# A graph network's sort pass: the work of three blocks woven turn by turn

## The chip, the cores and the metric

The kernel runs on one core of one Trainium2 chip. The metric is the time of one execution on the device in microseconds (us), the median of several runs. The program uses the five engines of the core: TensorE (PE in the profile, PEld for its weight loads), VectorE (DVE), ScalarE (ACT), GpSimd (POOL) and SyncE (SP), which issues most transfers.

## The reference, cut to what matters

Four graph layers run one after the other on 12,500 nodes and 412,500 edges, sorted by their target `dst`. The change concerns the first message layer alone:

```
def _L0_gnn_ref(node_features, edge_attr_e3nn, ..., edge_index):
    row, col = edge_index[0], edge_index[1]        # src, dst
    x_j = node_features[col]
    m = jnp.einsum('ei,ej,ijh->eh', x_j, edge_attr_e3nn, W_msg_tp) * norm_msg_tp
    m = jax.nn.silu(m)
    m = m @ W_msg_lin * norm_lin
    agg = jax.ops.segment_sum(m, row, num_segments=n_nodes)
    ...
```

Each edge takes its target's features, multiplies them with its eight attributes and the weights, passes through silu, and is added to its source. The later layers read the same edges again.

## The kernel before, in words

`sorted_message` is the sort pass. It computes the messages of this layer, and it also sorts the edges by source and writes the sorted lists that all later edge passes load. The edges come in 104 blocks (`BLOCKS`) of 128 lanes by 31 columns. A node pass ahead of it has multiplied the weights into a table of 128 values per node, so that a message is a gathered row of the table, times the eight attributes, summed over them.

A block goes through these steps, and each engine has its own function for a step, called `place`, `message` and `sum_`:

- `place` (VectorE L838 to L925). From `src` and `dst` each edge gets a cell, one of 34, by its source (L846 to L866). `hot_c` is the one-hot of the cells. `hot_d` (L875) is the one-hot of the target inside a window of 128 nodes, made in eight turns of four columns (`TURNS`). TensorE counts the cells (L1102) and transposes each turn of `hot_d` (L1111) into one bank, `ps_turn`; ScalarE copies it out (L1032). L877 to L901 find the rank of an edge within its cell, with products of 31 by 31; edges past 128 in a cell spill, TensorE counts these (L1114), and L904 to L925 turn rank and cell into a place.
- `message`. TensorE gathers each turn with a matmul of the transposed one-hot and the window (L1125), into two banks in turn. VectorE multiplies with the attributes (L937, one per turn) and sums over them (L943). ScalarE applies silu (L1045) into the record. GpSimd then scatters the records, 31 indirect transfers (L809), one column each, to the sorted places in HBM, and one more for the spills of an earlier block (L823).
- `sum_`. SP loads the sorted slots back (L762) once the scatter has landed, and then, for a later block, the edges' ends (L733 to L735). VectorE splits the messages by three chunks (`thirds`, L951 to L966), makes four groups of one-hots (`HOTS`, L973), and finds repeated spill rows (L977 to L989). TensorE turns two columns of the slots into rows (L1141, L1142), and adds the messages to their sources with 33 products (L1146, each two matmuls), and three more small ones (L1152 to L1156). ScalarE makes a second set of one-hots for the later passes, four groups of Square and Relu (L1063, L1067), and copies the sums out (L1073).

`in_pairs` unrolls the first six blocks and then loops over pairs. In turn k each of these three engines does `place(k)`, then `message(k - 1)`, then `sum_(k - 3)`. The order inside an engine is written out by hand; engines wait for one another by semaphore counts (`Chain` gives each step of each block its number), and a wait holds all that stands behind it on its engine. GpSimd's turn b waits for the index and for the silu of block b. SP's turn k loads the ends of block k, the attributes and the window, clears the records, stores what block k - 4 has ready, and waits for the scatter of block k - 2 to land before it loads its slots.

A copy of the numbers 0 to 127, `ps_iota`, stands in a PSUM bank that also holds accumulators of the first three sum cells; `iota128` is the same in SBUF. The one-hots compare with one of the two.

Of the kernel before, what the change touches and what calls it, by code (L numbers as in the profile page):

```python
# [26 lines left out]
LANES = 128  # L27
# [14 lines left out]
F = 16  # L42
# [68 lines left out]
def _gnn(nc, ctx, ins, out):  # L111
# [491 lines left out]
    def sorted_message(name, table, agg_src, agg_dst, agg_spill):  # L603
# [4 lines left out]
        with ExitStack() as st:  # L608
# [228 lines left out]
            def _(dve):  # L837
                def place(k, x, before):  # L838
# [33 lines left out]
                    if before:  # L872
                        dve.wait_ge(at_.sem, at_.end(k - 1))
                    for t, e in TURNS:
                        dve.tensor_tensor(hot_d[:, t:e, :], bc3(dlo[x][:, t:e], [LANES, e - t, LANES]),  # L875
                                          ps_iota[0:LANES, :].unsqueeze(1).broadcast_to([LANES, e - t, LANES]), ALU.is_equal).then_inc(av.sem, 1)
# [24 lines left out]
                    dve.tensor_reduce(within[:, :], pair[:, :, :], axis=AX.X, op=ALU.add).then_inc(av.sem, 1)  # L901
                    dve.wait_ge(av.sem, av.at("sooner_sum", k))
# [24 lines left out]
                def message(k, x, before):  # L927
# [4 lines left out]
                    dve.wait_ge(attrs_in[x], attrs_of(k, x))  # L932
                    for j, (t, e) in enumerate(TURNS):
                        dve.wait_ge(ct.sem, ct.at(f"gathered{j}", k))
                        if before and j == 0:
                            dve.wait_ge(cv.sem, cv.end(k - 1))
                        dve.tensor_tensor(prod[:, t:e], ps_y[j % 2][0:LANES, 0:(e - t) * AF].rearrange("p (t f a) -> p t f a", f=F, a=A),  # L937
                                          attrE[x][:, t * A:e * A].rearrange("p (t a) -> p t a", a=A).unsqueeze(2)
                                          .broadcast_to([LANES, e - t, F, A]), ALU.mult).then_inc(cv.sem, 1)
# [5 lines left out]
                def sum_(k, x, before):  # L945
# [14 lines left out]
                    message_ = s[:, :, 11:11 + F]  # L960
                    dve.tensor_tensor(thirds[:, :, 2, :], message_, bc3(top[:, :], [LANES, CELLS, F]), ALU.mult).then_inc(bv.sem, 1)
                    dve.tensor_tensor(thirds[:, :, 1, :], message_, bc3(upper[:, :], [LANES, CELLS, F]), ALU.mult).then_inc(bv.sem, 1)
                    dve.wait_ge(bv.sem, bv.at("high", k))
                    dve.tensor_tensor(thirds[:, :, 0, :], message_, thirds[:, :, 1, :], ALU.subtract).then_inc(bv.sem, 1)
                    dve.wait_ge(bv.sem, bv.at("middle", k))
                    dve.tensor_tensor(thirds[:, :, 1, :], thirds[:, :, 1, :], thirds[:, :, 2, :], ALU.subtract).then_inc(bv.sem, 1)  # L966
                    if before >= 2:
                        dve.wait_ge(lists_out[x], per_parity(k, x, 48, -48))
                    for g, (c, e) in enumerate(HOTS):
# [3 lines left out]
                        dve.tensor_tensor(hot[:, c:e, :], bc3(lower[:, c:e], [LANES, e - c, LANES]),  # L973
                                          numbers.unsqueeze(1).broadcast_to([LANES, e - c, LANES]), ALU.is_equal).then_inc(bv.sem, 1)
# [51 lines left out]
            def _(act):  # L1026
# [7 lines left out]
                def message(k, x, before):  # L1034
# [8 lines left out]
                    act.activation(rec[x][:, :, 3:3 + A], attrE[x][:, :].rearrange("p (t a) -> p t a", a=A), ACT.Copy).then_inc(cs.sem, 1)  # L1043
                    act.wait_ge(cv.sem, cv.at("summed", k))
# [3 lines left out]
                def sum_(k, x, before):  # L1048
# [8 lines left out]
                    for g, (c, e) in enumerate(HOTS):  # L1057
                        if g:
                            act.wait_ge(bs.sem, bs.at(f"target{g - 1}", k))
                        elif before:  # L1060
                            act.wait_ge(bs.sem, bs.end(k - 1))
                        for n in range(c, e):
                            last = act.activation(away[:, n - c, :], iota128[:, :], ACT.Square, scale=-1.0, bias=slots[x][:, n, 1:2])  # L1063
                        last.then_inc(bs.sem, 1)
                        act.wait_ge(bs.sem, bs.at(f"away{g}", k))
                        act.activation(ready_[:, :], lane[:, 0:1], ACT.Copy).then_inc(bs.sem, 1)
                        act.activation(targets_[x][:, c * LANES // 2:e * LANES // 2].bitcast(FP8), away[:, 0:e - c, :].rearrange("p c l -> p (c l)"), ACT.Relu,  # L1067
                                       scale=-1.0, bias=1.0, saturate=False).then_inc(bs.sem, 1)
# [27 lines left out]
            def _(pe):  # L1096
                def place(k, x, before):
# [6 lines left out]
                    for j, (t, e) in enumerate(TURNS):  # L1104
                        pe.wait_ge(av.sem, av.at(f"hot_d{j}", k))
                        if j:
                            pe.wait_ge(as_.sem, as_.at(f"turned_out{j - 1}", k))
                        elif before:
                            pe.wait_ge(as_.sem, as_.at(f"turned_out{len(TURNS) - 1}", k - 1))
                        for n in range(t, e):  # L1110
                            mm = pe.matmul(ps_turn[:, (n - t) * LANES:(n - t + 1) * LANES], hot_d[:, n, :], ident16[:, :], start=True, stop=True)  # L1111
                        mm.then_inc(at_.sem, 1)
# [3 lines left out]
                def message(k, x, before):  # L1116
                    pe.wait_ge(attrs_in[x], attrs_of(k, x))
                    pe.wait_ge(as_.sem, as_.end(k))
                    for j, (t, e) in enumerate(TURNS):
                        if j >= 2:  # L1120
                            pe.wait_ge(cv.sem, cv.at(f"prod{j - 2}", k))
                        elif before:
                            pe.wait_ge(cv.sem, cv.at(f"prod{len(TURNS) - 2 + j}", k - 1))
                        for n in range(t, e):
# [2457 lines left out]
```

## Time and profile before

| What | Value |
|---|---|
| Median of 3 runs | 18172.39 us (18166.81 to 18178.23) |
| The profiled execution | 18176.88 us, span 18175.2 us |
| Busy over the span | PE 14091.7, DVE 13399.8, ACT 7133.0, POOL 4607.0 us |
| Mean granted clock of TensorE | 0.814 |
| Sort pass, 1000 to 2000 us of the span | PE 700, DVE 836, ACT 492, POOL 722 us of 1000, clock 0.61 |

The sort pass fills about the stretch from 430 to 5280 us; the first product sum is at 477.0 and the last at 5200.9. Behind it come the node passes and the other edge passes. "Busy" doesn't count waits, semaphore instructions and issue. A granted clock of 1.00 is TensorE's 2.4 GHz level, 0.50 its 1.2 GHz level. A wait is put down to the engine and line whose event came last.

### The profile page before, as it was taken

The page shows a single profiled execution, that of the slowest core. Times are in us where ns is not written, and L with a number is a line of the kernel's source. Part 1 is how long each engine was busy: PE and PEld are TensorE (multiplying, and loading weights), DVE is VectorE, ACT ScalarE, POOL GpSimd, SP SyncE. Part 2 cuts the span into 40 slices and gives each one's busy share as a digit, 9 for nine tenths or more (in the row PEclk, how much of TensorE's full clock was granted, in tenths as well). Part 3 has the DMA queues.
Part 4 walks back from the last instruction along what each step waited for, and adds up shares of the span by engine and source line. Part 5 has one row for each costly group of instructions (what it writes and reads, how often), then busy time and mean ns, then how long its engine had stood idle before and what let it go on. Part 6 is the DMA issues. An engine that isn't in the chain of part 4 may idle for free. (4 is left out here: it accounts for less than half of the span.)

```text
span 18175.2 us, 508933 instructions
## 1 busy us (share of the span) xinstructions
PE 14091.7 (78%) x180600; PEld 12229.2 (67%) x180600; DVE 13399.8 (74%) x32882; ACT 7133.0 (39%) x15316; POOL 4607.0 (25%) x4403
## 2 busy tenths in 40 slices
PE   1676677677667995899999999997699999946565
PEld 0566666666656994777777777776577777736565
DVE  2888888888857995656666666665677777769899
ACT  0444445444432332344444444443344444411111
POOL 0677777777741110011111111110000000001111
PEclk9666666666657996999999999998899999967676
DMA  1122222222213551444444444443344444427566
GB/s 58 53 59 59 58 57 59 59 59 58 59 48 112 156 157 56 107 110 110 110 110 110 110 110 111 110 110 83 108 151 151 151 152 152 144 70 210 169 210 178
DMA packets 1347425, 1956.50 MB, mean 108 GB/s; under 512 B 705453, under 2 KB 923252, under 8 KB 1306316
## 3 DMA queue, kind: packets, MB, share of 16 engines
q1 hardware_dynamic: 1046674, 1621.50, 28.8%
q0 software_dynamic: 209664, 186.01, 7.2%
q10 hardware_dynamic: 90300, 137.10, 2.0%
q8 instruction: 666, 10.91, 0.2%
q14 instruction: 121, 0.99, 0.0%
HBM read 1443.57 MB, written 501.97 MB: 107 GB/s over the span
## 5 line engine op out<-in xcount | busy, mean ns | idle before, releaser
L809 POOL DMA_INDIRECT records<-e_sort_rec,e_sort_index x3224 | 3293.2, 1021 | 1351.1 <-issue 921.2
L2393 PEld LDWEIGHTS e_s_ps_h<-e_s_pick,e_s_parts 128*64 128x64 bf16 x61776 | 2044.1, 116 | 215.7 <-issue 67.6
L2393 PE MATMUL e_s_ps_h<-e_s_pick,e_s_parts 128*64 128x128 bf16 x61776 | 2095.7, 227 | 13.7 <-issue 13.6
L1146 PE MATMUL e_sort_acc<-e_sort_thirds,e_sort_hot 128*128 128x48 f32 x6864 | 1488.7, 414 | 301.0 <-DVE e_sort_hot L973 301.0
L1146 PEld LDWEIGHTS e_sort_acc<-e_sort_thirds,e_sort_hot 128*128 128x128 f32 x6864 | 1472.0, 332 | 331.6 <-DVE e_sort_hot L973 331.6
L2512 POOL DMA_DIRECT2D states<-e_s_second_t x520 | 457.8, 880 | 4603.1 <-ACT e_s_second_t L2241 4531.4
L2029 DVE TENSOR_TENSOR e_s_unit<-e_s_ps_o,lane_out 128x512 f32<-128x512 f32 (+1 forms) x520 | 324.0, 623 | 1720.8 <-PE e_s_ps_o L2351 1720.8
L1989 DVE TENSOR_SCALAR e_s_pick<-e_s_rows,lane_below 128x1024 bf16<-128x1024 bf16 (+1 forms) x3120 | 1178.9, 434 | 232.3 <-PE e_s_ps_h L2393 208.3
L2426 PE MATMUL e_s_ps_o<-w_eblk,e_s_act 128*128 128x128 f32 x7488 | 1018.8, 277 | 210.6 <-DVE e_s_unit L2038 210.6
L2503 POOL DMA_INDIRECT e_s_spill<-send,e_s_lists x208 | 218.5, 1050 | 3677.0 <-PE e_s_ps_h L2415 2757.2
L2426 PEld LDWEIGHTS e_s_ps_o<-w_eblk,e_s_act 128*128 128x128 f32 x7488 | 952.3, 192 | 276.9 <-DVE e_s_unit L2038 230.4
L1063 ACT ACTIVATE e_sort_away<-iota,e_sort_slots 128x128 f32<-128x128 f32 x3640 | 1107.5, 388 | 10.1
L1125 PE MATMUL e_sort_y<-e_sort_window,e_sort_turned 128*128 128x128 f32 x6448 | 997.9, 325 | 11.6 <-DVE e_sort_prod L937 7.5
L1125 PEld LDWEIGHTS e_sort_y<-e_sort_window,e_sort_turned 128*128 128x128 f32 x6448 | 952.3, 234 | 44.6 <-DVE e_sort_prod L937 21.6
L2386 PE MATMUL e_s_ps_h<-e_s_to_hot,e_s_window 128*64 128x512 bf16 (+2 forms) x6240 | 866.9, 383 | 110.0 <-DVE e_s_to_hot L1990 96.1
L2214 ACT ACTIVATE e_s_act<-e_s_ps_h,col_eenc 128x512 f32<-128x512 f32 (+1 forms) x520 | 335.3, 645 | 1533.6 <-PE e_s_ps_h L2342 1533.6
L2453 PE MATMUL e_s_ps_sum<-e_s_unit,e_s_wide 128*128 128x128 f32 x7280 | 899.3, 275 | 0.1
L1111 PE MATMUL e_sort_turn<-ident,e_sort_hot_d 128*128 128x128 bf16 x3224 | 491.6, 306 | 506.0 <-ACT e_sort_turned L1032 498.8
L1400 PE MATMUL e_s_g<-e_s_parts,e_s_pick 128*128 128x48 bf16 x20592 | 768.3, 205 | 120.9 <-DVE e_s_pick_own L1296 64.7
L2453 PEld LDWEIGHTS e_s_ps_sum<-e_s_unit,e_s_wide 128*128 128x128 f32 x7280 | 855.1, 192 | 0.7 <-issue 0.7
L2248 ACT ACTIVATE e_s_act<-e_s_ps_h,col_state 128x512 f32<-128x512 f32 (+1 forms) x1040 | 663.4, 638 | 462.3 <-PE e_s_ps_h L2412 257.5
L1691 PE MATMUL e_s_psp<-e_s_wide,e_s_product 128*128 128x128 f32 x7280 | 839.3, 276 | 3.6 <-DVE e_s_product L1591 3.1
(546 smaller groups left out, 31707.8 us busy)
## 6 DMA issues: line engine op xcount, KB each, us to landing
e_s_rows<-rows_d SPq DMA_DIRECT2D x312, 1088.0 KB, 5.3
e_s_hot<-hots_d SPq DMA_DIRECT2D x520, 560.0 KB, 3.7
e_s_to_rows<-rows_d SPq DMA_DIRECT2D x208, 608.0 KB, 5.7
e_s_rows<-rows_d SPq DMA_DIRECT2D x208, 544.0 KB, 4.3
e_s_rows<-rows_d SPq DMA_DIRECT2D x208, 512.0 KB, 5.2
e_s_to_rows<-rows_d SPq DMA_DIRECT2D x208, 512.0 KB, 6.0
states<-e_s_first_t ACTq DMA_DIRECT2D x416, 256.0 KB, 2.1
states<-e_s_second_t POOLq DMA_DIRECT2D x416, 256.0 KB, 4.0
```

The source lines that it names most:

```text
L809: pool.indirect_dma_start(records, bass.IndirectOffsetOnAxis(ap=index[x][:, t:t + 1], axis=0), rec[x][:, t, :], None,).then_inc(written[x] ...
L1063: last = act.activation(away[:, n - c, :], iota128[:, :], ACT.Square, scale=-1.0, bias=slots[x][:, n, 1:2])
L1125: mm = pe.matmul(ps_y[j % 2][0:LANES, (n - t) * AF:(n - t + 1) * AF], turned[x][:, n, :], window[x][:, :], start=True, stop=True)
L1146: mm = pe.matmul(acc[sum_bank(c)][:, sum_at(c)], hot[:, c, :], thirds[:, c, :, :].rearrange("p h f -> p (h f)"), start=False, stop=last an ...
L1400: mm = pe.matmul(ps_g[g][:, at:at + 3 * F], pick[x][:, h, c * LANES:(c + 1) * LANES], parts[:, SPAN * c + h, :, :].rearrange("p r f -> p ( ...
L1691: mm = pe.matmul(ps_spread[:, 0:LANES], product[x][:, c].rearrange("p a f -> p (a f)"), wide[:, c * LANES:(c + 1) * LANES], start=c == 0, ...
L1989: dve.tensor_scalar(pick[p][:, h, 0:(f - c) * LANES], rows_[:, c * LANES:f * LANES], lane_below[:, h:h + 1], None, ALU.is_equal).then_inc( ...
L2248: act.activation(act1[p][:, 0:turned(s)], hidden_bank(x, s)[:, 0:turned(s)], ACT.Silu, bias=(col_state if enc else col_state1)[:, :]).then ...
L2386: pe.matmul(halves[half][:, 0:n_ * LANES], window[:, r, 1, :], to_pairs[:, half, 0:n_, :], start=r == 0, stop=False, skip_group_check=True)
L2393: mm = pe.matmul(halves[half][:, j * LANES:(j + 1) * LANES], parts[:, SPAN * c + h, r, :], pick[p][:, h, (c - c0) * LANES:(c - c0 + 1) * L ...
L2426: mm = pe.matmul(ps_o1[p % NB][:, j * LANES:(j + 1) * LANES], act1[p][:, j * LANES:(j + 1) * LANES], W[f"eblk1{rnd}"][:, :], start=enc, st ...
L2453: mm = pe.matmul(ps_sum[:, 0:2 * D if enc else D], wide[s][:, (c - c0) * LANES:(c - c0 + 1) * LANES], units_of(x, c), start=c == 0, stop=F ...
```

## The change

The three step functions of VectorE, ScalarE and TensorE are cut into pieces, and the loop bodies call the pieces in a new order. On TensorE each turn gathers block k - 1 and then transposes block k. On VectorE each turn makes a target one-hot of block k and a product of block k - 1, and six of the eight turns also take a piece of the sums of block k - 3. The ranks and places of block k stand at the end. On ScalarE the copies into the record come first, and the silu stands between the second and the third group of target one-hots. One-hot group 2 of the sums reads `iota128` in place of `ps_iota`, and the wait for the first accumulations moves from group 2 to group 3. TensorE's wait for the spill rank moves behind the sums. The same instructions run as before, and the programs of SP and GpSimd are not touched.

```
VectorE:
+                def sum_hot(k, x, g, before):
+                    c, e = HOTS[g]
+                    numbers = iota128[:, :] if g in (1, 2) else ps_iota
+                    if g == 3:
+                        dve.wait_ge(bt.sem, bt.at("early", k))
+                    dve.tensor_tensor(hot[:, c:e, :], bc3(lower[:, c:e], [LANES, e - c, LANES]),
+                                      numbers.unsqueeze(1).broadcast_to([LANES, e - c, LANES]), ALU.is_equal).then_inc(bv.sem, 1)
...
-                        numbers = iota128[:, :] if g == 1 else ps_iota
-                        if g == 2:
-                            dve.wait_ge(bt.sem, bt.at("early", k))
...
                 def body(k, x, before):
                     y = 1 - x
-                    if inside(k):
-                        place(k, x, before)
-                    if before >= 1 and (not isinstance(k, int) or k - 1 < BLOCKS):
+                    new, sent, summed_ = inside(k), before >= 1 and (not isinstance(k, int) or k - 1 < BLOCKS), before >= 3
+                    if new:
+                        cells_(k, x, before)
+                    if sent:
+                        indices(k - 1, y, before - 1)
+                    for j in range(len(TURNS)):
+                        if new:
+                            target_hot(k, x, j, before)
+                        if sent:
+                            products(k - 1, y, j, before - 1)
+                        if summed_ and j == 1:
+                            thirds_low(k - 3, y, before - 3)
+                        if summed_ and j == 2:
+                            thirds_top(k - 3, y, before - 3)
+                        if summed_ and j == 3:
+                            thirds_rest(k - 3, y, before - 3)
+                        if summed_ and j in (4, 5, 6):
+                            sum_hot(k - 3, y, j - 4, before - 3)
+                    if sent:
                         message(k - 1, y, before - 1)
-                    if before >= 3:
-                        sum_(k - 3, y, before - 3)
+                    if summed_:
+                        sum_hot(k - 3, y, 3, before - 3)
+                        spill_rows(k - 3, y, before - 3)
+                    if new:
+                        ranks(k, x, before)
+                        places(k, x, before)
ScalarE:
-                    if inside(k):
+                    if sent:
+                        message(k - 1, y, before - 1)
+                    if new:
                         place(k, x, before)
-                    if before >= 1 and (not isinstance(k, int) or k - 1 < BLOCKS):
-                        message(k - 1, y, before - 1)
-                    if before >= 3:
+                    if summed_:
                         sum_(k - 3, y, before - 3)
+                        targets(k - 3, y, 0, before - 3)
+                        targets(k - 3, y, 1, before - 3)
+                    if sent:
+                        silu_(k - 1, y, before - 1)
+                    if summed_:
+                        targets(k - 3, y, 2, before - 3)
+                        targets(k - 3, y, 3, before - 3)
+                        sums(k - 3, y, before - 3)
TensorE:
-                        pe.wait_ge(av.sem, av.at("spill_rank", k + 3))
...
+                def sum_spills(k, x, before):
+                    if not last_of_places(k):
+                        pe.wait_ge(av.sem, av.at("spill_rank", k + 3))
...
-                    if inside(k):
-                        place(k, x, before)
-                    if before >= 1 and (not isinstance(k, int) or k - 1 < BLOCKS):
-                        message(k - 1, y, before - 1)
-                    if before >= 3:
+                    for j in range(len(TURNS)):
+                        if sent:
+                            message(k - 1, y, j, before - 1)
+                        if new and j == 0:
+                            count(k, x, before)
+                        if new:
+                            turn(k, x, j, before)
+                    if summed_:
                         sum_(k - 3, y, before - 3, isinstance(k, int) and k == BLOCKS + 2)
+                    if new:
+                        spills(k, x, before)
+                    if summed_:
+                        sum_spills(k - 3, y, before - 3)
```

The new functions hold the lines of the old ones unchanged but for what is shown here: on VectorE `cells_`, `target_hot`, `ranks` and `places` are the parts of `place`; `indices`, `products` and `message` those of `message`; `thirds_low`, `thirds_top`, `thirds_rest`, `sum_hot` and `spill_rows` those of `sum_`.

## Rows read from the trace of the kernel before

**Rows 1.** product sum L943 over the stage: count, duration ns, first and last start
```profile
L943 DVE TENSOR_REDUCE e_sort_summed<-e_sort_prod x104: 4285/4286/4287, 477.0 to 5200.9; 128x496 f32<-128x3968 f32 x104
```

**Rows 2.** waits, 500 to 5200: us in total, times, longest
```profile
DVE e_sort_spill_rank L904 <- PE e_sort_misc L1114: 348.7, 100, 4.3
POOL records L809 <- ACT e_sort_rec L1045: 334.1, 102, 5.0
...
DVE e_sort_prod L937 <- PE e_sort_y L1125: 227.1, 569, 11.7
...
DVE e_sort_dlo L846 <- issue: 34.8, 49, 1.4
```

**Rows 3.** groups of GpSimd, 1000 to 5000: busy us, mean ns, idle before
```profile
L809 POOL DMA_INDIRECT records<-e_sort_rec,e_sort_index x2691 | 2750.6, 1022 | 1083.9 <-issue 767.6 <-ACT e_sort_rec L1045 290.4 <-DVE e_sort_index L931 25.9
L823 POOL DMA_INDIRECT agg<-e_sort_merged,e_sort_spill_at x87 | 140.0, 1610 | 26.5 <-issue 26.5
```

**Rows 4.** timeline of VectorE, one block: start us, us
```profile
3004.28 0.18 DVE L951 TENSOR_SCALAR e_sort_upper<-e_sort_slots 128x35 f32<-128x35 f32 x1
...
3009.36 1.35 DVE L973 TENSOR_TENSOR e_sort_hot<-e_sort_lower,iota 128x1152 f32<-128x1152 f32 x1
...
3015.24 0.19 DVE L846 TENSOR_TENSOR e_sort_dlo<-e_sort_dst,e_sort_first 128x31 f32<-128x31 int32 x1
...
3018.29 4.73 DVE L875 TENSOR_TENSOR e_sort_hot_d<-e_sort_dlo,e_sort_acc 128x512 bf16<-128x512 f32 x8
3022.94 1.15 DVE L877 TENSOR_TENSOR e_sort_pair<-e_sort_cell 128x961 f32<-128x961 f32 x1
...
3036.00 0.19 DVE L904 TENSOR_TENSOR e_sort_spill_rank<-e_sort_within,e_sort_misc 128x31 f32<-128x31 f32 x1 [3.70 <-PE e_sort_misc L1114]
...
3038.54 0.69 DVE L937 TENSOR_TENSOR e_sort_prod<-e_sort_y,e_sort_attr 128x512 f32<-128x512 f32 x1
```

**Rows 5.** timeline of TensorE, the same blocks
```profile
3004.81 1.07 PE L1141 MATMUL e_sort_turn<-ident,e_sort_slots 128*35 128x128 f32 x4 [5.45 <-DVE e_sort_diagonal L953]
3005.80 0.80 PE L1142 MATMUL e_sort_turn<-e_sort_diagonal,ones 128*128 128x128 f32 x2
3009.50 14.31 PE L1146 MATMUL e_sort_acc<-e_sort_thirds,e_sort_hot 128*128 128x48 f32 x66 [2.90 <-DVE e_sort_hot L973]
...
3025.47 1.06 PE L1102 MATMUL e_sort_misc<-e_sort_hot_c,earlier 128*128 128x34 bf16 x31 [0.43 <-ACT e_sort_merged L1073]
...
3027.64 0.61 PE L1111 MATMUL e_sort_turn<-ident,e_sort_hot_d 128*128 128x128 bf16 x4 [0.69 <-ACT e_sort_turned L1032]
...
3082.20 3.45 PE L1125 MATMUL e_sort_y<-e_sort_window,e_sort_turned 128*128 128x128 f32 x16
```

**Rows 6.** windows: stretch; PE, PEld, DVE, ACT, POOL busy; clock; DMA share; GB/s
```profile
3085.80:3091.60 5.80, 5.71 (x46) 5.36 (x46) 4.06 (x7) 0.00 (x0) 4.34 (x5) 1.00 0.05 11
```

**Rows 7.** timeline of ScalarE: silu and two target groups
```profile
3004.40 0.65 ACT L1045 ACTIVATE e_sort_rec<-e_sort_summed 128x496 f32<-128x496 f32 x1 [12.94 <-DVE e_sort_summed L943]
...
3006.92 2.72 ACT L1063 ACTIVATE e_sort_away<-iota,e_sort_slots 128x128 f32<-128x128 f32 x9
...
3010.96 2.74 ACT L1063 ACTIVATE e_sort_away<-iota,e_sort_slots 128x128 f32<-128x128 f32 x9
```

**Rows 8.** timelines of GpSimd, SP, VectorE, second round; GpSimd at block of group 4
```profile
521.88 0.95 POOL L809 DMA_INDIRECT records<-e_sort_rec,e_sort_index  x1 [0.31 <-issue]
...
526.56 0.43 SPq L735 DMA_DIRECT2D e_sort_first<-firsts_d  x1
...
529.19 0.19 DVE L846 TENSOR_TENSOR e_sort_dlo<-e_sort_dst,e_sort_first 128x31 f32<-128x31 int32 x1 [15.76 <-DMA e_sort_first<-firsts_d]
...
557.07 4.29 DVE L943 TENSOR_REDUCE e_sort_summed<-e_sort_prod 128x496 f32<-128x3968 f32 x1
...
558.55 0.96 POOL L809 DMA_INDIRECT records<-e_sort_rec,e_sort_index  x1 [0.30 <-issue]
...
3009.81 1.74 POOL L809 DMA_INDIRECT records<-e_sort_rec,e_sort_index  x1 [0.30 <-issue]
```

More of the change, by code:

```diff
@@ L837, in _, with cells_ @@
             def _(dve):
-                def place(k, x, before):
+                def cells_(k, x, before):
                     src_, dst_ = srcE[x][:, :], dstE[x][:, :]
@@ L901, in place, with places @@
                     dve.tensor_reduce(within[:, :], pair[:, :, :], axis=AX.X, op=ALU.add).then_inc(av.sem, 1)
+                def places(k, x, before):
                     dve.wait_ge(av.sem, av.at("sooner_sum", k))
@@ L931, in message, with products @@
                     dve.tensor_copy(index[x][:, :], place_[x][:, :]).then_inc(cv.sem, 1)
[L932 to L939, printed above, removed]
+                def products(k, x, j, before):
+                    t, e = TURNS[j]
+                    if j == 0:
+                        dve.wait_ge(attrs_in[x], attrs_of(k, x))
+                    dve.wait_ge(ct.sem, ct.at(f"gathered{j}", k))
+                    if before and j == 0:
+                        dve.wait_ge(cv.sem, cv.end(k - 1))
+                    dve.tensor_tensor(prod[:, t:e], ps_y[j % 2][0:LANES, 0:(e - t) * AF].rearrange("p (t f a) -> p t f a", f=F, a=A),
+                                      attrE[x][:, t * A:e * A].rearrange("p (t a) -> p t a", a=A).unsqueeze(2)
+                                      .broadcast_to([LANES, e - t, F, A]), ALU.mult).then_inc(cv.sem, 1)
+                def message(k, x, before):
                     dve.wait_ge(cv.sem, cv.at(LAST, k))
@@ L1056, in sum_, with targets, sums @@
                     act.activation(rows_t[x][:, :], ps_rows, ACT.Copy).then_inc(bs.sem, 1)
[L1057 to L1068, printed above, removed]
+                def targets(k, x, g, before):
+                    c, e = HOTS[g]
+                    if g:
+                        act.wait_ge(bs.sem, bs.at(f"target{g - 1}", k))
+                    elif before:
+                        act.wait_ge(bs.sem, bs.end(k - 1))
+                    for n in range(c, e):
+                        last = act.activation(away[:, n - c, :], iota128[:, :], ACT.Square, scale=-1.0, bias=slots[x][:, n, 1:2])
+                    last.then_inc(bs.sem, 1)
+                    act.wait_ge(bs.sem, bs.at(f"away{g}", k))
+                    act.activation(ready_[:, :], lane[:, 0:1], ACT.Copy).then_inc(bs.sem, 1)
+                    act.activation(targets_[x][:, c * LANES // 2:e * LANES // 2].bitcast(FP8), away[:, 0:e - c, :].rearrange("p c l -> p (c l)"), ACT.Relu,
+                                   scale=-1.0, bias=1.0, saturate=False).then_inc(bs.sem, 1)
+                def sums(k, x, before):
                     act.wait_ge(bt.sem, bt.at("merged", k))
@@ L1096, in _, with count @@
             def _(pe):
-                def place(k, x, before):
+                def count(k, x, before):
                     pe.wait_ge(av.sem, av.at("hot_c", k))
@@ L1103, in place, with turn @@
                     mm.then_inc(at_.sem, 1)
[L1104 to L1112, printed above, removed]
+                def turn(k, x, j, before):
+                    t, e = TURNS[j]
+                    pe.wait_ge(av.sem, av.at(f"hot_d{j}", k))
+                    if j:
+                        pe.wait_ge(as_.sem, as_.at(f"turned_out{j - 1}", k))
+                    elif before:
+                        pe.wait_ge(as_.sem, as_.at(f"turned_out{len(TURNS) - 1}", k - 1))
+                    for n in range(t, e):
+                        mm = pe.matmul(ps_turn[:, (n - t) * LANES:(n - t + 1) * LANES], hot_d[:, n, :], ident16[:, :], start=True, stop=True)
+                    mm.then_inc(at_.sem, 1)
@@ L1113, in place, with spills, message @@
+                def spills(k, x, before):
                     pe.wait_ge(av.sem, av.at("lates16", k))
                     pe.matmul(ps_lates, earlier16[:, :], lates16[:, :], start=True, stop=True).then_inc(at_.sem, 1)
[L1116 to L1124, printed above, removed]
[L1125 to L1127 removed]
+                def message(k, x, j, before):
+                    t, e = TURNS[j]
+                    if j == 0:
+                        pe.wait_ge(attrs_in[x], attrs_of(k, x))
+                        pe.wait_ge(as_.sem, as_.end(k))
+                    if j >= 2:
+                        pe.wait_ge(cv.sem, cv.at(f"prod{j - 2}", k))
+                    elif before:
+                        pe.wait_ge(cv.sem, cv.at(f"prod{len(TURNS) - 2 + j}", k - 1))
+                    for n in range(t, e):
+                        mm = pe.matmul(ps_y[j % 2][0:LANES, (n - t) * AF:(n - t + 1) * AF], turned[x][:, n, :], window[x][:, :],
+                                       start=True, stop=True)
+                    mm.then_inc(ct.sem, 1)
```

30 lines of the change are left out of this document (17 added, 13 removed).

## The prediction, made before the run

> **What bounds the kernel now.** The change touches one stage only, the sort pass, so I read that stage and left the chain that ended last aside: it lies wholly in the last node pass. First the spacing of one instruction that runs once for each of the 104 blocks, the product sum at L943 [rows 1]: 103 steps from 477.0 to 5200.9, 45.86 us each. The stage is 4724 us of 18175, so one microsecond off a block is worth 103 us, 0.57% of the kernel.
>
> Then the waits [rows 2], to see which engine is ever full. VectorE waits 3.45 us a block (348.7 over 101 blocks) at L904 for TensorE and 2.25 (227.1) at its products; GpSimd waits 3.3 for ScalarE's silu. Nobody is full: the three take turns in one ring. L846 to L875 makes one-hots, TensorE transposes only when the previous block's sums are through, the gathers come after that, and VectorE's sums after the gathers.
>
> Last, how near each engine is to its own limit. GpSimd [rows 3]: 87 rounds in the stretch, 31 scatters of 1.022 us, one spill of 1.61, and 9.43 us of idle time that is only issue (767.6 + 25.9 + 26.5 over 87). That is 42.72, and the wait for silu, 290.4/87 = 3.34, fills it to 46.06. So GpSimd leaves at most 3.0 us a block to be gained, because a round that waits for nothing still pays one issue step of 0.30. VectorE: 46.06 less its two waits is 40.4.
>
> **What the change does, part by part.** No instruction is added or removed; the order on VectorE, ScalarE and TensorE changes, and one of four sum one-hots (group 2) compares with iota128 in SBUF, where it read the copy in PSUM. SP's and GpSimd's programs stay.
>
> *VectorE with TensorE.* I lay one turn of the new loop along durations of before, from L846 at 0. Cells and the chunk one-hot end at 3.05 (3015.24 to 3018.29) [rows 4], the index cast at 3.25 (L904 to the first product, 2.54, holds the places and this cast; I give the cast 0.2), the first target one-hot (0.58: 4.65 for eight, L875 to L877) at 3.85. TensorE starts its count at 3.1, ends it at 4.2 (1.06), transposes four columns (0.61) until 4.8, and only then, because its queue is in order, gathers group 1. A group of gathers costs 3.45/2 = 1.73 [rows 5], so product 1 can start at 6.5. VectorE is there at 5.1 (two one-hots, one product of 0.69): a stall of 1.4. From turn 1 on each turn also holds a piece of the sums: a third of L951 to L973 (5.08 less one one-hot of 1.35 is 3.7, so 1.25 each) or a sum one-hot. VectorE's turn is then 0.58 + 0.69 + 1.25 = 2.5 and TensorE's 1.73 + 0.61 = 2.34, so VectorE hardly waits; I take 0.2 in all. The product sum (4.29 [rows 1]) ends near 26.5, the fourth one-hot and the spill rows near 29.4, the ranks (L877 to L904, 13.06 less the 3.70 of waiting) near 38.8. TensorE meanwhile: last transpose 22.3, ScalarE's copy 0.7 (the wait ahead of L1111), rows 1.07 + 0.80, sums 14.31, so the spill count comes at 39.2: a stall of 0.4 where 3.45 stood. The places add 2.3 and the loop's jump 0.35 (34.8 of idle time at L846 over 101 blocks [rows 2]): 41.9. By parts it is 40.4 + 1.4 + 0.2 + 0.4 = 42.4. I take 42.0. Bounds of this unknown: 40.4 with no stall, and 1.4 in each of eight turns, 40.4 + 11.2 + 0.4 = 52.0. I stand near the low end, because only turn 0 has no filler between its two products.
>
> I took the slow gather. In a long run of gathers the granted clock stood at 1.00, the 2.4 GHz level, and 46 of them took 5.71 us, 0.124 each [rows 6]; the 16 ahead of them took 3.45, 0.216 each [rows 5]. Woven between transposes and waits the long run is gone. The Trainium skill, "TensorE: Matmul & The Clock Gate", Part 1, says the same as a rule: the throttled clock is the default and sustained activity releases it. By the fast rate TensorE's turn would be 1.0 + 0.6 and the first stall 0.7; VectorE's round would be 41.2 where I have 42.0. Neither sets the end of the sum, as GpSimd will show below.
>
> *ScalarE.* The silu moves behind two groups of target one-hots, 4.04 each (L1063 to the next L1063) [rows 7]. TensorE's rows are there at 24.9 (22.3 + 0.7 + 1.9), so silu (0.65) ends near 24.9 + 8.1 + 0.7 = 33.7, 7 us after its input is there. I give GpSimd 0.7 more to start: 34.4 after L846. Does that hold GpSimd up? When round b ends, SP loads slots and then the next ends, and VectorE may start block b+3. The second round at the start of the stage shows this path: last scatter at 521.88, L735 issued at 526.56, VectorE released at 529.19 [rows 8], 6.4 us after the scatter ended (521.88 + 0.96). The silu follows 34.4 later, 40.8 after the scatter's end, less the spill of 1.9 that ends the round, while GpSimd is busy for 43 with the other block. So it is 2 to 4 us early, and GpSimd goes from round to round. VectorE's spare time will then stand at L846.
>
> *GpSimd is what is late next.* Its round without the silu wait is 42.72 + 0.30 = 43.02. But part of 1.022 is collision. A scatter alone takes 0.96 (558.55); the one at 3009.81 took 1.74 and ended 0.84 after the one-hot with iota128 in SBUF (3009.36 + 1.35 = 3010.71) [rows 4, 8]. The 4.29 us product sum delays nothing: the scatter at 558.55 lies inside the one at 557.07. So operations with two SBUF inputs hold GpSimd, and reductions don't; 31 x (1.022 - 0.96) = 1.9 us a block goes there now. The change adds to this. Group 2 becomes a second 1.35 us blocker, longer than a scatter's step of 1.26, so it always catches one: between 0.09 and 1.35, middle 0.72. And the first pair of thirds, which ran while GpSimd sat waiting for silu, now meets a busy GpSimd: between nothing and 0.74, I take 0.3. GpSimd's own loop jump, hidden so far under the silu wait, is between nothing and VectorE's 0.35; I take 0.15. Round after: 43.02 + 0.72 + 0.30 + 0.15 = 44.2.
>
> The Trainium skill, "SBUF — State Buffer", "Who interferes with whom", states this as a rule that speaks against the change: a VectorE instruction with two SBUF inputs takes the port that GpSimd reads through, for its whole length, and a reduction never does. The trace agrees in both halves, by the 1.74 and the 0.96 above. By the rule alone, each of the blockers could cost its full length.
>
> **Sum.** 103 x 44.2 = 4553 against 4724: 171 us less. Fill and drain keep their work, and the stages behind are untouched. The profiled execution took 18176.9 (span 18175.2), 4.5 above the median of 18172.4, so 18172.4 - 171 = 18001; I say 18,000.
>
> **Rivals.**
> - *GpSimd binds as computed*, with 43.0 to 45.4 a block: 17,878 to 18,125. Chance 0.68.
> - *Few collisions.* If the blockers fall between GpSimd's reads (those measured now are 1.9 of some 6 possible), the VectorE and TensorE ring binds, down to 42.0: 103 x 3.86 = 398 less, 17,775. Against it: the 1.35 us blockers are longer than one step. Chance 0.12.
> - *The weave itself stalls.* Where VectorE and TensorE wait for each other in all eight turns, x more in each, a block takes 42.0 + 8x. It shows from x = 0.28 and ends slower than before from x = 0.53; at the bound of 52.0 a block it is 103 x 6.1 = 630 us more, 18,800. Against it: every turn but the first has a filler longer than the transposes. Chance 0.08.
> - *Slower by the port.* Every blocker caught at its start: two one-hots (2.7), two of the three 1.15 us pair operations (2.3), one of each pair of thirds (1.5), 6.5 a block in place of 1.9: 43.02 + 4.6 + 0.15 = 47.8, 103 x 1.9 = 196 more, 18,370. It decides from 5.1 of collisions. For it: the order repeats each block, so a bad phase repeats too. Against: the same blockers now cost 1.9. Chance 0.07.
> - *The silu stays the wait.* If ScalarE reaches it 4 us later than laid out (rows held up by TensorE), GpSimd waits as now and a block stays at 45.5 to 46.2, the time within 0.2%: 18,172. Chance 0.05.
>
> **Numbers.** A difference of 0.2%, 36 us or 0.35 us a block, is about what a measurement can tell. Faster: 0.68 + 0.12 + 0.03 + 0.01 + 0.01 of the five cases, 0.85; within it: 0.02 + 0.02 + 0.03, 0.07; slower: 0.03 + 0.04 + 0.01, 0.08. The range 17,850 to 18,125 holds the first case and the upper part of the second; below it lies 0.08, above it some 0.12.
>
> **What would show it.** Right: L943 every 44.2 us; GpSimd's wait for ScalarE near nothing and its scatters at a mean of 1.05 to 1.06; VectorE's idle time moved from L904 to L846, behind the load of the ends, some 2 us; the gathers at the slow rate throughout. Wrong: waits at every product (the weave), scatters above 1.12 (the port), or GpSimd still waiting 3 us for silu.

## The result, and the profile after

The changed kernel took 17,838.94 us (17,832.56 to 17,847.32, four runs) against 18,171.61 before (18,166.81 to 18,178.23): a ratio of 0.9816, 95% interval 0.9801 to 0.983. It is faster, by nearly twice the 171 us of the prediction, and lies 11 us below the low end of its range. The profiled span is 17,833.8 us. The same kernel run again in a later comparison gave 17,825.87 (17,797.54 to 17,833.18), 0.9799 [0.9783, 0.9816].

The product sum, now at L954, answers to [rows 1]: one line of its own view, with count, durations in ns, first and last start.

```profile
L954 DVE TENSOR_REDUCE e_sort_summed<-e_sort_prod x104: 4285/4286/4287, 463.6 to 4844.8; 128x496 f32<-128x3968 f32 x104
```

A block takes (4844.8 - 463.6)/103 = 42.54 us, where it took 45.86 and 44.2 was forecast. That is 342 us over 103 blocks, as much as the two profiled spans differ (18175.2 and 17833.8): the stage gave all of it.

The waits from 500 to 4900 us (total, times, longest) and the groups of GpSimd from 1000 to 4500 answer to [rows 2] and [rows 3]:

```profile
DVE e_sort_dlo L846 <- DMA e_sort_first<-firsts_d: 182.6, 89, 6.1
DVE e_sort_prod L946 <- PE e_sort_y L1186: 160.8, 103, 1.6
...
DVE e_sort_spill_rank L910 <- PE e_sort_misc L1174: 20.6, 47, 0.8
POOL records L809 <- ACT e_sort_rec L1088: 11.9, 39, 0.3
```

```profile
L809 POOL DMA_INDIRECT records<-e_sort_rec,e_sort_index x2538 | 2557.1, 1008 | 773.2 <-issue 754.6 <-ACT e_sort_rec L1088 9.4 <-DVE e_sort_prod L946 9.1
L823 POOL DMA_INDIRECT agg<-e_sort_merged,e_sort_spill_at x82 | 146.8, 1790 | 25.0 <-issue 25.0
```

GpSimd no longer waits: its longest "wait" for silu, 0.3, is the issue step that stands ahead of every scatter. Its round is 31 x 1.008 + 1.79 + (773.2 + 25.0)/82 = 31.2 + 1.8 + 9.7 = 42.8, the whole block (42.76 in this stretch; the first blocks of the stage are shorter). VectorE's 3.45 for the spill count has shrunk to 0.2, its waits for gathers from 2.25 to 1.6, and it now idles 1.8 us a block at L846, behind the load of the ends. What differs most from the forecast is the scatters: a mean of 1.008 us, lower than before's 1.022, not 1.05 to 1.06.

The timelines of GpSimd and VectorE in one block show why (start, duration; [rows 4, 8] before):

```profile
3011.67 1.57 POOL L809 DMA_INDIRECT records<-e_sort_rec,e_sort_index  x1 [0.30 <-issue]
3013.55 0.96 POOL L809 DMA_INDIRECT records<-e_sort_rec,e_sort_index  x1 [0.31 <-issue]
...
3027.68 0.96 POOL L809 DMA_INDIRECT records<-e_sort_rec,e_sort_index  x1 [0.30 <-ACT e_sort_rec L1088]
3028.94 1.61 POOL L823 DMA_INDIRECT agg<-e_sort_merged,e_sort_spill_at  x1 [0.30 <-issue]
3030.86 0.97 POOL L809 DMA_INDIRECT records<-e_sort_rec,e_sort_index  x1 [0.30 <-issue]
...
3011.07 1.35 DVE L989 TENSOR_TENSOR e_sort_hot<-e_sort_lower,iota 128x1152 f32<-128x1152 f32 x1
...
3013.53 1.41 DVE L989 TENSOR_TENSOR e_sort_hot<-e_sort_lower,iota 128x1152 f32<-128x1152 f32 x1
...
3026.77 0.63 ACT L1088 ACTIVATE e_sort_rec<-e_sort_summed 128x496 f32<-128x496 f32 x1
```

The first one-hot with `iota128` catches the scatter that starts inside it: it ends at 3013.24, 0.82 after the one-hot's end (3011.07 + 1.35 = 3012.42). The next scatter starts 0.30 later, at 3013.55, and so 0.02 after the second such one-hot. This one it passes: it takes its 0.96, and the one-hot took 1.41 where its like took 1.35. The silu stands complete at 3027.40, 3.5 us ahead of the next round's start at 3030.86.

The pass is not certain. From 1000 to 4500 us, 58 scatters started 0.015 to 0.026 us after the second one-hot; 43 of them passed, and 15 were caught for its whole length, as this one, with its one-hot below it:

```profile
1003.52 2.16 POOL L809 DMA_INDIRECT records<-e_sort_rec,e_sort_index  x1 [0.30 <-issue]
...
1003.50 1.34 DVE L989 TENSOR_TENSOR e_sort_hot<-e_sort_lower,iota 128x1152 f32<-128x1152 f32 x1
```

### The profile page after: what moved, and what is told of

Its sections match the earlier page's. It is cut to its first block and busy times, and to the rows that moved or that the text cites. A ratio compares the mean times of both kernels' runs of the same rounds, so it can differ in the third digit from the quotient of the medians.

```text
span 17833.8 us, 508622 instructions
## 1 busy us (share of the span) xinstructions
PE 14016.7 (79%) x180289; PEld 12267.5 (69%) x180600; DVE 13331.9 (75%) x32882; ACT 7108.2 (40%) x15316; POOL 4569.4 (26%) x4403
## 5 line engine op out<-in xcount | busy, mean ns | idle before, releaser
L809 POOL DMA_INDIRECT records<-e_sort_rec,e_sort_index x3224 | 3247.7, 1007 | 1034.6 <-issue 957.8
L1206 PE MATMUL e_sort_acc<-e_sort_thirds,e_sort_hot 128*128 128x48 f32 x6864 | 1443.6, 405 | 6.8 <-DVE e_sort_hot L989 6.8
L1073 ACT ACTIVATE e_sort_turned<-e_sort_turn 128x512 f32<-128x512 f32 x832 | 486.2, 584 | 1985.9 <-PE e_sort_turn L1169 1975.7
L1186 PE MATMUL e_sort_y<-e_sort_window,e_sort_turned 128*128 128x128 f32 x6448 | 1238.3, 352 | 2.8 <-DVE e_sort_prod L946 2.7
L1186 PEld LDWEIGHTS e_sort_y<-e_sort_window,e_sort_turned 128*128 128x128 f32 x6448 | 1107.8, 258 | 3.7 <-DVE e_sort_prod L946 3.5
```

Source lines behind the costliest of these rows:

```text
L809: pool.indirect_dma_start(records, bass.IndirectOffsetOnAxis(ap=index[x][:, t:t + 1], axis=0), rec[x][:, t, :], None,).then_inc(written[x] ...
L1186: mm = pe.matmul(ps_y[j % 2][0:LANES, (n - t) * AF:(n - t + 1) * AF], turned[x][:, n, :], window[x][:, :], start=True, stop=True)
L1206: mm = pe.matmul(acc[sum_bank(c)][:, sum_at(c)], hot[:, c, :], thirds[:, c, :, :].rearrange("p h f -> p (h f)"), start=False, stop=last an ...
```

## The experiments

Theory A: GpSimd's round sets the block; a collision re-times the scatters behind it, so collisions don't add. Its rivals: B, each operation with two SBUF inputs costs its own 0.72 on top; C, the ring of VectorE and TensorE still sets the block; D, lateness of the silu counts in full (E and F, where an expectation names them, are variants of how much of it a round can take); G, GpSimd bound the kernel before, too; H, the gain is from the ranks' place alone. Ratios are to the kernel before on the same chip.

**Is GpSimd the bound, and since when?** Three runs give it fewer of the 31 columns, and SP the smaller count of landings to wait for, and change nothing else: `range(30)` and `range(27)` in the changed kernel, `range(29)` in the one before. The records of the other columns stay empty, so part of the edges is left out of the result.

```
-                    for t in range(BLOCK_T):
+                    for t in range(30):
```

> The changed kernel without the scatter of column 30 of each block: 30 of 31 columns are sent, and the records of the last stay empty, which leaves part of the edges out. Theory A (GpSimd's round sets the block): one step of 1.26 us less, 130 us, 17,710. Theory C (VectorE and TensorE set it): no change, 17,840.

> The changed kernel with 27 of 31 columns scattered (four columns of each block are left out). GpSimd's round would be 5.0 us shorter, 37.5, so the VectorE and TensorE ring shows itself. Theory A: VectorE waits 1.8 us a block at the load of the ends now, so its ring is 40.7 to 41.2: 140 to 190 us less, 17,650 to 17,700. By the ring of 42.0 that the forecast had: 55 us less, 17,785. If GpSimd were all: 518 us less, 17,320.

> The kernel before, with 29 of 31 columns scattered (two columns of each block are left out). Theory A: before the change the ring of VectorE, TensorE and ScalarE sets the block and GpSimd waits 3.3 us for silu, so nothing is gained: 18,172 within 20 us, and GpSimd's wait grows by 2.5 us a block. Rival G (GpSimd's round already set the block before): 2.5 us a block less, 17,910.

With 30 columns: 17,658.44 us, 0.9711 [0.9695, 0.9727], 40.86 us a block (462.7 to 4671.2). One step of 1.26 us less gave 1.68, the rest being fewer collisions (scatters at 0.998, the spill at 1.61). Had the ring set the block, a scatter less would have changed nothing, so C falls. VectorE no longer waits for the loads at L846 in this run: with 30 columns the ring is already met. With 27: 17,661.62, 0.9712 [0.9696, 0.9728], 41.06 a block, no faster than 30. Now GpSimd waits for silu, 184.4 us over 85 rounds, and the ring shows itself at 41 (forecast 42.0). The kernel before with two columns less: 18,169.75, 0.9992 [0.9982, 1.0001]. Its wait for silu grew from 3.3 to 5.9 us a round (445.9 over 76) and nothing else moved, so G falls: before, GpSimd followed. Its group there (1000 to 4500):

```profile
L809 POOL DMA_INDIRECT records<-e_sort_rec,e_sort_index x2204 | 2261.9, 1026 | 1094.7 <-issue 625.6 <-ACT e_sort_rec L1045 445.9 <-DVE e_sort_index L931 23.2
```

**What does a collision cost?** Three runs change which one-hots of the sums read SBUF, or where they stand: none (with TensorE's first groups waiting for one-hot 2, as the PSUM bank of `ps_iota` demands), three, and the two of the change with no turn between them.

```
-                    numbers = iota128[:, :] if g in (1, 2) else ps_iota
+                    numbers = ps_iota                          # none
+                    numbers = iota128[:, :] if g in (0, 1, 2) else ps_iota   # three
```
```
+                        if summed_ and j == 6:                 # hot 2 ahead of product 6
+                            sum_hot(k - 3, y, 2, before - 3)
                         ...
-                        if summed_ and j in (4, 5, 6):
+                        if summed_ and j in (4, 5):
```

> The changed kernel, but all four sum one-hots compare with the numbers in PSUM, so none of them reads two SBUF operands; TensorE's first sums wait for the third one-hot, which is long done by then. Theory A (GpSimd's round sets the block, 42.54 us, and a caught scatter re-times the train behind it): one of the two 1.35 us one-hots is caught now, for about 0.65 us (scatters of 1.57 and 1.65 where 0.96 is usual), the other slips by. Both gone: 0.3 to 0.7 us a block less, 17,765 to 17,810. Theory B (each blocker costs its own 0.72, whatever the others do): 1.4 a block less, down to the VectorE ring: about 17,695. Theory C (VectorE and TensorE set the block): no change, 17,840.

> The changed kernel, with a third sum one-hot (group 0) on the numbers in SBUF. Group 0 starts 2.47 us ahead of group 1, two scatter steps less 0.06. Theory A: a scatter caught by group 0 puts the next one at the start of group 1, so the three cost hardly more than the two: within 35 us of 17,840. Theory B: 0.72 a block more, 74 us, 17,913. Theory C: no change.

> The changed kernel, with the third sum one-hot ahead of product 6 and not behind it, so that it starts 0.6 us sooner after the second. Theory A: the scatter that now starts just as the third one-hot starts is then caught within it: 0.4 to 0.75 us a block more, 17,880 to 17,917, and a second scatter of about 1.6 us in each round. Theory B: spacing doesn't matter, no change, 17,840. Theory C: product 6 is 1.35 later, nothing waits for it, no change.

None: 17,782.08, 0.978 [0.9763, 0.9796], 42.04 us a block. Three: 17,844.12, 0.9811 [0.9795, 0.9827], 42.83. Two side by side: 17,993.69, 0.9892 [0.9875, 0.9908], 44.08, more than A expected. The last one moves one instruction of 1.35 us past one of 0.69 and loses 155 us (138 by the ratios). That is a matter of phase; here are GpSimd and VectorE of that kernel:

```profile
3013.47 1.82 POOL L809 DMA_INDIRECT records<-e_sort_rec,e_sort_index  x1 [0.30 <-issue]
3015.60 1.56 POOL L809 DMA_INDIRECT records<-e_sort_rec,e_sort_index  x1 [0.30 <-issue]
...
3013.12 1.35 DVE L989 TENSOR_TENSOR e_sort_hot<-e_sort_lower,iota 128x1152 f32<-128x1152 f32 x1
...
3014.98 1.35 DVE L989 TENSOR_TENSOR e_sort_hot<-e_sort_lower,iota 128x1152 f32<-128x1152 f32 x1
```

A caught scatter ends 0.82 to 0.83 after its blocker, and the next starts 0.30 behind that: 1.13 after the blocker's end. In the change the second one-hot starts 1.11 after the first ends (3012.42 to 3013.53), so that scatter falls on its start and mostly passes. Here it starts 0.51 after (3014.47 to 3014.98), and the scatter at 3015.60 lands inside it and pays 0.60.

In the table, the time of every scatter over 0.962 us (of the spill over 1.61) is added up from the timelines of 2000 to 3800 us, by the operation in which it started, and divided by the rounds (us a block). The first pair of the ranks is the product at L881 (L877 before), the late pair the one at L902 (L898), the thirds L974 to L982 (L961 to L966):

| Started in | before | changed | none | three | side by side |
|---|---|---|---|---|---|
| one-hots with `iota128` | 0.78 | 0.84 | 0 | 1.23 | 1.24 |
| ranks, first pair | 0.41 | 0.21 | 0.85 | 0.22 | 0.73 |
| ranks, late pair | 0.62 | 0.12 | 0 | 0.20 | 0.52 |
| the pairs of thirds | 0.14 | 0.25 | 0.27 | 0.30 | 0.62 |
| all | 1.95 | 1.43 | 1.13 | 1.97 | 3.22 |

So B falls: with a second blocker the one-hots cost 0.06 more than before, with the third another 0.39, and taking both away gave only 0.30 of their 0.84 back, because the first pair of the ranks then caught its scatter near its start, for 0.85 in place of 0.21. Side by side, the one-hots themselves cost only 0.40 more than in the change; the pairs of the ranks, re-timed, cost 0.92 more and the thirds 0.37. The column sums, on a round of 31 x 0.962 + 1.61 + 9.73 = 41.2, give 42.6, 42.3, 43.1 and 44.4 for the last four, in the order of the measured 42.54, 42.04, 42.83 and 44.08 and within 0.3 of them.

How often the second one-hot passes its scatter differs along the stage. From 1000 to 4500 us the changed kernel's column adds up to 1.64 (one-hots 0.92, ranks 0.21 and 0.19, thirds 0.30), that of before to 1.96 and that of none to 1.17. There the second blocker added 0.14, and taking both away gave 0.47, close to the 0.50 that a block lost. A run of the change with `ps_iota` in group 2 alone was not made.

**How late may the silu be?** It stands behind two of four target groups of ScalarE; here behind three, then behind four.

```
                     if summed_:
                         targets(k - 3, y, 1, before - 3)
+                        targets(k - 3, y, 2, before - 3)
+                        targets(k - 3, y, 3, before - 3)       # second run only
                     if sent:
                         silu_(k - 1, y, before - 1)
```

> The changed kernel, with ScalarE's silu behind three groups of target one-hots, 4.05 us later. Theory A: 4.05 less the 3.5 us that silu is early now, halved: 0.3 us a block more, about 17,870, between 17,840 and 17,900. Rival D (counted in full): 0.6 a block, 17,900. Rival F (silu's place already sets the block): 4.05 a block, 18,255.

> The changed kernel, with ScalarE's silu behind all four groups of target one-hots, 8.1 us later. In the trace silu now ends 3.5 us before GpSimd needs it (3027.40 against 3030.86). The path from a round's end through the loads, VectorE and silu spans two rounds, so what it is late counts half. Theory A: 8.1 less 3.5, halved: 2.3 us a block more, GpSimd waits for ScalarE again, about 18,075. Rival D (the wait counts in full in every round): 4.6 a block, 18,310. Rival E (silu has slack to spare): no change, 17,840.

Behind three: 17,910.71, 0.9848 [0.9832, 0.9864], 43.25 a block, 0.71 more than the change; of it 0.56 are waits for silu (45.1 us over 80 rounds). It fits neither forecast well and decides nothing by itself. Behind four: 18,064.2, 0.9932 [0.9915, 0.9949], 44.92 a block, as A said and half of what D said. The waits of VectorE and GpSimd there (1000 to 4500):

```profile
DVE e_sort_dlo L846 <- DMA e_sort_first<-firsts_d: 320.6, 60, 9.6
...
POOL records L809 <- ACT e_sort_rec L1083: 191.0, 39, 5.4
```

L1083 is a small copy that starts right behind the silu, which sets the wait. The wait comes in every second round, 39 times in 78: the delay goes round a loop of two blocks. VectorE's block starts at L846, the silu starts 40.2 us later, GpSimd 1.45 after it, its 31 scatters last 40.6, and the next L846 of this loop stands 7.5 after their end, behind SP's loads: 89.8 us, 44.9 a block. In the change L846 to silu is 32.4 and the scatters last 40.4, so the loop would allow 40.9; behind three groups, with 36.6 to the silu, it allows 43.1, close to the 43.25 measured.

**Does VectorE's own time matter?** The version without `iota128` again, with the 31 by 31 products of the ranks in bf16 where the values are 0 and 1 (`pair`, `late` and a bf16 copy of `sooner`).

> The run with all sum one-hots on PSUM, and also the 31 by 31 products of the ranks held as bf16 zeros and ones (pair, late and the mask), exact as before. Two of the three pair operations read 16-bit operands and may take half as long, so they block GpSimd less. Theory A: GpSimd's round without a collision is 31 scatters of 0.96 and 11.4 us of spill and issue, 41.2; it stood at 42.04 with the one-hots on PSUM, with 0.85 of that in collisions with the first pair operation, which stays. Between 41.3 and 42.1 a block, 70 to 150 us below the changed kernel. Theory B (each blocker pays for itself): the two shorter ones save 0.2 to 0.5 us each. Theory C: VectorE is 1.1 us a block shorter, all of it gained.

17,780.06, 0.9776 [0.976, 0.9793]. Two products fell from 1.16 to 0.67 us each, VectorE has 1 us a block more, and the time is that of the version in f32 (0.978): spare time of VectorE is worth nothing now.

**Which part of the order gave the gain?** First the weave alone undone: all transposes, then all gathers; on VectorE all target one-hots, the pieces of the sums, then all products; ranks and places stay last. Then ranks and places put back to where they stood, ahead of the sums and products, with the spill count right behind the transposes.

```
-                    for j in range(len(TURNS)):      # TensorE: gather turn j, count, transpose turn j
+                    for j in range(len(TURNS)):      # all count and transposes
+                        ...
+                    for j in range(len(TURNS)):      # then all gathers
+                        if sent:
+                            message(k - 1, y, j, before - 1)
```
```
                         for j in range(len(TURNS)):
                             target_hot(k, x, j, before)
+                        ranks(k, x, before)
+                        places(k, x, before)
```

> The changed kernel without the weave itself: TensorE transposes all eight turns of the new block and then gathers all eight of the block before, VectorE makes all target one-hots, then the pieces of the sums, then all products; ranks and places stay last and ScalarE's order stays. Theory A, by the same timetable: transposes end at 14.6 after the start of a turn, gathers at 24.5, sums at 40.7, spill count 40.9, so the VectorE ring is 43.5 to 44.6 a block and sets it, GpSimd waits 1 to 2 us for silu: 100 to 210 us over the changed kernel. Rival H (ranks and places last is what counts, the weave adds nothing): equal to the changed kernel.

> The changed kernel as it is, beside the others on the same chip: a ratio to before of 0.980 to 0.983 as measured at first; all theories agree.

> The unwoven version with one thing moved back to where the kernel before had it: ranks and places stand ahead of the sums' pieces and the products on VectorE, and the spill count stands right behind the transposes on TensorE. If the place of the ranks is what took the long wait out of the ring of VectorE and TensorE, that wait is back: some 3.4 us a block at L910, and with the unwoven version's 43.05 us a block, of which 3.1 are waits, a block takes 45.2 to 46.0 us, and the time is 18,110 to 18,190, GpSimd waiting 2 to 3 us a block for silu. If the gain came from the early copies, the early index or the silu's place instead, a block stays near 43 us and the time within 40 us of 17,887.

Unwoven: 17,887.13, 0.9838 [0.9822, 0.9855], 43.05 a block, 61 us more than the changed kernel beside it. This is less than A expected, and not nothing as H did. VectorE waits 2.7 us at the products (221.6 over 81 blocks) and hardly at L846, so the ring sets the block again, at 43.05 where the weave has 41.06; but GpSimd's round, 42.54 in the change, hides most of that gain.

Ranks put back as well: 18,366.27, 1.0101 [1.0085, 1.0118], 47.51 a block (476.0 to 5369.6), slower than the kernel before, and above the 18,110 to 18,190 expected. In the new order, then, all of the gain needs the ranks' place, as H has it in the main, but by another wait than the expectation named. VectorE's and GpSimd's waits there (1000 to 4500):

```profile
DVE e_sort_dlo L846 <- DMA e_sort_first<-firsts_d: 304.7, 74, 5.0
...
POOL records L809 <- ACT e_sort_rec L1088: 342.3, 74, 5.3
```

No wait at L910 is listed. The ranks now stand between L846 and the products, and the loop of two blocks has become the bound. Its timelines of VectorE, ScalarE and GpSimd:

```profile
3011.96 0.19 DVE L846 TENSOR_TENSOR e_sort_dlo<-e_sort_dst,e_sort_first 128x31 f32<-128x31 int32 x1 [3.49 <-DMA e_sort_first<-firsts_d]
...
3048.82 4.29 DVE L954 TENSOR_REDUCE e_sort_summed<-e_sort_prod 128x496 f32<-128x3968 f32 x1
...
3057.41 0.63 ACT L1088 ACTIVATE e_sort_rec<-e_sort_summed 128x496 f32<-128x496 f32 x1
...
3058.86 0.97 POOL L809 DMA_INDIRECT records<-e_sort_rec,e_sort_index  x1 [4.17 <-ACT e_sort_rec L1088]
```

From L846 to the silu it is 45.45 us (45.2 in the mean of nine blocks) in place of 32.4: 45.2 + 1.45 + 41.2 + 7.5 = 95.4, 47.7 a block, against 47.51 measured.

The ranks stood there in the kernel before, too, and the silu came 35.0 us after L846. The other 10 us belong to the rest of the new order: the pieces of the sums now stand ahead of the products (the product sum starts 36.8 us after L846, 30.6 before), and the silu waits for ScalarE's two target groups (4.3 us after the product sum's end, where before it followed at once). So this run doesn't split the gain over the kernel before; no run moves the ranks alone in that kernel, and H's "alone" is not shown.

## Why the prediction was right, and where it failed

Right, by its own steps:
- *What bounds.* Before, no engine was full and VectorE and TensorE took turns; the run of before with 29 columns shows that GpSimd only followed. "GpSimd is what is late next" is shown by the run with 30 columns.
- *The stalls.* The first product waits 1.56 to 1.60 (1.4 forecast), later turns nothing (0.2), the spill count 0.2 (0.4). The ring is 41.06, not 42.0. It sets no end, but "few collisions" could have gone to 41.
- *The silu* is early by 3.5 us (2 to 4 forecast), and the loop from L846 over silu, scatter and loads was reckoned with the right members; the two runs with a later silu, and the last run, show it bind as soon as it is lengthened.
- VectorE's idle time went to L846, 1.8 us (some 2).

The step that failed is "Round after: 43.02 + 0.72 + 0.30 + 0.15 = 44.2". It took the 1.9 us of collisions that were there as fixed and added the price of new blockers. Measured, from 1000 to 4500 us, were 1.64 in place of 1.9 + 1.02. The one-hots cost 0.14 more rather than 0.72, since the first one sets the next scatter on the second's start, where most pass; the thirds cost 0.15 more rather than 0.30; and the pairs of the ranks lost 0.62, because the new order put them at other phases. That GpSimd's loop jump would show (0.15) was also wrong: every issue gap is 0.3. Together (2.92 - 1.64) + 0.15 = 1.43 us a block, 147 us of the 161 between 18,000 and the result.

A smaller slip is in the sum: it set 44.2, a round of the steady stretch, against 45.86, the mean of all steps. The first ten steps before took 44.96 each and the steady ones 46.06, so this made the forecast gain 0.2 us a block, some 20 us, too small.

The outcome lies between the prediction's first case and "few collisions": collisions did become fewer, which it gave 0.12, but GpSimd still binds. That this order's phases are good ones is luck, as one instruction moved gives 17,994. What stays open is whether the phases of all 32 transfers could have been forecast from the rows of before; the prediction did not try, and so had no ground for the sign of this term.

The rule of the Trainium skill that was weighed, in "SBUF — State Buffer", "Who interferes with whom", also says that the order of issue, not the operation, decides which of the two engines is blocked. The trace agrees for scatters that start well inside a blocker: they all end behind it. For starts 0.02 us apart the recorded order doesn't tell, since 43 scatters passed and 15 did not; and a one-hot that let a scatter pass took 1.41 for 1.35, so it was held for 0.06 and not for the scatter's 0.96. For a train of scatters the phases shown above decide.

"The gathers at the slow rate throughout" was wrong, and as the ring is not the bound it didn't decide the time. TensorE's timeline shows eight gathers in 2.02 us and in 1.11 within one block:

```profile
2998.57 2.02 PE L1186 MATMUL e_sort_y<-e_sort_window,e_sort_turned 128*128 128x128 f32 x8
...
3003.24 1.11 PE L1186 MATMUL e_sort_y<-e_sort_window,e_sort_turned 128*128 128x128 f32 x8
...
```

The granted clock over the gathers just before the second eight shown, and then over these, is the value behind the five busy times in a line of windows (the length, then PE, PEld, DVE, ACT, POOL busy, clock, DMA share, GB/s). TensorE had stood idle for 3.58 us before 2997.30 and had then worked until 3002.84:

```profile
3000.90:3002.80 1.90, 1.90 (x10) 1.64 (x8) 1.86 (x8) 0.60 (x1) 1.29 (x3) 0.50 0.29 90
3003.30:3004.30 1.00, 1.00 (x10) 0.86 (x8) 1.00 (x3) 0.60 (x1) 0.70 (x2) 1.00 0.03 6
```

The change is named for its weave, but without the weave the new order loses only some 60 us. Its ranks' place is worth the most, 479 us between the unwoven version and the last run: behind the products, the ranks no longer lie on the way to the silu. That it also took the wait for the spill count out of the ring is not shown, since that wait is missing with the ranks ahead, too. The version without `iota128` beats both kernels, at 0.978.

## What to carry to other kernels

When a change takes the slack from an engine that issues one transfer after another, its collisions with another engine are not a sum of prices but a matter of phase: give them a range of both signs around what they cost now, and try to take the blockers away (here one operand in PSUM, some 50 us). Before moving a step, follow the loop that it lies on over all engines and blocks, with its period in blocks: a delay in a loop of two blocks costs half of itself, and nothing while the loop is shorter than the busiest engine's round. An engine that idles at one wait may be held by a loop elsewhere; leaving out some of its work, as in the runs with fewer columns, tells at once whether it is the bound.

## What the runs showed of the hardware

- A scatter that starts within a VectorE operation with two SBUF inputs, and would end sooner, is held until 0.82 to 0.85 us after that operation (1.57, 1.82, 1.56 and 2.16 us here, 0.96 alone). Of those that start about 0.02 us after the operation did, 43 of 58 went through in 0.96 and 15 were caught. With one input in PSUM the same one-hot delayed no scatter. In the unwoven version the short TENSOR_SCALAR at L970, with one SBUF tensor and one value per lane as inputs, caught 11 scatters in the same way.
- Short runs of gathers between waits do reach TensorE's 2.4 GHz level: eight took 1.11 us at a granted clock of 1.00 in some turns, 2.02 at 0.50 in others. With the gathers unwoven the following sums ran at a mean of 314 ns a matmul, woven at 407; what that is worth in time no run here shows.
